# Own bank for turned rows, a bias moved to VectorE, an earlier second routing and earlier keys in the first expert layer

## The reference, cut to what matters

```python
xf = layernorm(x).reshape(-1, 128)                       # 4096 tokens
scores = sigmoid(xf @ Wg.T + bg + bias)                  # 8 experts
top_scores, top_idx = top_k(scores, 2)
h  = gelu(einsum('td,ehd->teh', xf, W1) + b1)            # hidden 512
eo = einsum('teh,edh->ted', h, W2) + b2
shared = gelu(xf @ Ws1.T + bs1) @ Ws2.T + bs2            # every token
x = x + shared + (eo weighted by the two scores)
...
kh = (ctx_1024 @ Wk + bk)                                # next layer's keys, 1601 rows a batch
```

## Time and profile before

| | us |
|---|---|
| median of 3 runs | 1750.25 (1744.02 to 1752.11) |
| the profiled execution, its own time | 1747.45 |
| its span | 1745.6 |
| layer B's front and shared expert | about 150 to 249 |
| the 46 units | about 249 to 490 |
| mean granted TensorE clock | 0.963 of full |

### The profile page before, as it was taken

The page is one execution under the profiler, slowest core; times in us unless marked ns, Lnnn a source line. Parts: engine busy times, 40 slices in busy tenths (PEclk is TensorE's granted clock), DMA queues, the critical chain, the costliest instruction groups (busy, mean ns, idle before and its releaser), DMA issues.

```text
span 1745.6 us, 44990 instructions
## 1 busy us (share of the span) xinstructions
PE 1508.3 (86%) x18392; PEld 923.6 (53%) x18392; DVE 1098.5 (63%) x2790; ACT 1255.9 (72%) x1537; POOL 353.3 (20%) x280
## 2 busy tenths in 40 slices
PE   3537987787789999999999999999988999999996
PEld 2436876676654545555454555445444555545553
DVE  6987245655554565667656465755578777778763
ACT  0453233443379999999999999999985677677664
POOL 7451754011050020201102020000001111221121
PEclk9767999998999999999999999999999999999998
DMA  8402112152233344434423343343200000000000
GB/s 306 149 1 68 52 55 65 49 127 58 56 86 74 72 105 92 93 84 91 95 65 80 91 105 90 74 90 68 83 4 1 7 1 7 7 7 7 7 1 13
DMA packets 71950, 112.75 MB, mean 65 GB/s; under 512 B 14656, under 2 KB 56896, under 8 KB 71360
## 3 DMA queue, kind: packets, MB, share of 16 engines
q1 hardware_dynamic: 65600, 95.09, 22.2%
q0 software_dynamic: 6144, 14.76, 2.7%
HBM read 41.36 MB, written 18.35 MB: 34 GB/s over the span
## 4 chain that ended last, share of the span: by engine, by line
PE 40%; ACT 23%; issue 14%; DVE 11%; POOL 1%; DVEq 1%; ACTq 0%; POOLq 0%
ACT C_probs L2195 20%; PE C_ps_s L1406 7%; PE C_ps_s L1415 7%; PE C_ps_s L858 6%; DVE C_den_t L2367 3%; PE C_ps_o L2090 3%; PE C_ps_o L1431 2%; PE C_ps_s L824 2%; PE C_ps_p L1396 2%; PE C_ps_s L2075 2%; ACT B_hidden L927 2%; PE C_ps_s L845 2%; POOL C_o_t L2240 1%; PE C_ps_s L813 1%; PE C_ps_p L2032 1%
## 5 line engine op out<-in xcount | busy, mean ns | idle before, releaser
L2195 ACT ACTIVATE C_probs<-C_ps_s 128x1024 f32<-128x1024 f32 x832 | 772.2, 1065 | 28.8 <-PE C_ps_s L2075 25.8
L2090 PE MATMUL C_ps_o<-C_probs,C_values 128*16 128x256 f32 x6656 | 440.0, 382 | 7.5 <-DVE C_o_t L2363 6.9
L1494 ACT ACTIVATE D_hidden<-C_ps_s,D_b_up 128x1024 f32<-128x1024 f32 x256 | 275.4, 1114 | 135.6 <-PE C_ps_s L1406 135.4
L2075 PE MATMUL C_ps_s<-C_queries,C_keys 32*128 32x256 f32 x3328 | 211.4, 328 | 26.8 <-ACT C_probs L2195 25.6
L2090 PEld LDWEIGHTS C_ps_o<-C_probs,C_values 128*16 128x16 f32 x6656 | 154.5, 95 | 145.8 <-ACT C_probs L2195 9.9
L2075 PEld LDWEIGHTS C_ps_s<-C_queries,C_keys 32*128 32x128 f32 x3328 | 126.8, 183 | 155.4 <-ACT C_probs L2195 117.7
L1406 PE MATMUL C_ps_s<-D_up_in,D_w_up_r 128*128 128x512 f32 x512 | 186.5, 446 | 2.0 <-ACT D_hidden L1494 2.0
L2240 POOL TENSOR_TENSOR C_o_t<-C_o_t,C_den_t 128x512 f32<-128x512 f32 x32 | 40.9, 1277 | 696.9 <-DVE C_den_t L2367 696.9
L858 PE MATMUL C_ps_s<-B_w_dn,B_hidden 128*128 128x128 f32 x736 | 100.5, 294 | 55.2 <-DVE B_unit_lo L1079 35.8
L1509 POOL TENSOR_TENSOR D_gated<-D_gated,D_gated 128x1024 f32<-128x1024 f32 x32 | 76.3, 2383 | 323.5 <-DVE D_gated L1634 323.5
L1415 PE MATMUL C_ps_s<-D_hidden,D_w_down 128*32 128x512 f32 x1024 | 137.7, 610 | 0.8 <-ACT D_hidden L1494 0.8
(11 more groups left out here) (309 smaller groups left out, 2302.2 us busy)
## 6 DMA issues: line engine op xcount, KB each, us to landing
C_keys<-C_k_hi SPq DMA_DIRECT2D x128, 200.1 KB, 4.1
C_ctx_t<-ctx_t_dram SPq DMA_DIRECT2D x16, 800.5 KB, 4.4
C_keys<-C_k_lo SPq DMA_DIRECT2D x64, 200.1 KB, 4.1
B_sorted_rows<-B_zeros SPq DMA_DIRECT2D x2, 2944.0 KB, 14.7
B_unit_in<-B_sorted_rows SPq DMA_DIRECT2D x46, 128.0 KB, 2.4
B_result_rows<-B_unit_out SPq DMA_DIRECT2D x46, 128.0 KB, 1.8
C_queries<-C_q_hi SPq DMA_DIRECT2D x128, 32.0 KB, 1.9
B_w_up<-L_ffn_w_up_dram SPq DMA_DIRECT2D x1, 2304.0 KB
```

The lines of the kernel that those rows point to most:

```text
L1494: nc.scalar.activation(hidden[:, u % RING, :, :], ps_u[u % 2][:], ACT.Gelu, bias=b_up[:, u % PAIRS:u % PAIRS + 1]).then_inc(s_hid, 1)
L2075: m = T.matmul(ps_s[bank(k, 2 * step + j // 2)][:, j % 2, i, :], keys[rows, parity, g, kt * P:(kt + 1) * P], queries[rows, parity, g, :], ...
L2090: m = T.matmul(ps_o[32 * j:32 * j + 2 * DK, g % 2, :], values[:, parity, kt, g * HG + j, :], probs[:, slot(parity, 2 * step + j // 2), j % ...
L2195: nc.scalar.activation(probs[:, slot(parity, n)], ps_s[bank(k, n)][:], ACT.Exp, scale=SCORE_SCALE1).then_inc(s_exp, 1)
```

## The change

Four things. (1) Turned rows of a unit go to the routing bank `ps_g`, and `turn_unit(v)` waits until VectorE has read unit v-1's; `down(v)` loses its wait on `s_us`, and its result moves to the free half of the bank. (2) `down_shared` loses the bias product; `add_shared` adds the bias on VectorE before it waits for the result. (3) Turned blocks 1 and 2 go to the two halves of `ps_s[2]`, `xt` has four places instead of two, the turns of blocks 4 to 7 come one block earlier, and so do their scores, ahead of `up_shared`; the second half's `choose` and `assign` come earlier on VectorE, and its `ranks` ahead of block 7's `up_shared`. `xt` and `unit_in` now share memory, so the first load of a unit waits for the last split and scores. (4) The key jobs move: 0 and 1 behind `down_shared(5)` and `(6)`, 2, 3 and 4 ahead of the units, 5 and 6 in units 2 and 3.

```diff
-    xt = over["keys1"]("xt", [P, 2, BT, P])
+    xt = [over[place](f"xt{i}", [P, BT, P]) for i, place in enumerate(("keys1", "keys1", "queries", "queries"))]
...
-    ps_t = ps_p[:].rearrange("p (i t) -> p i t", i=BT)
+    ps_t = [bank.rearrange("p (i t) -> p i t", i=BT) for bank in (
+        ps_p[:], *(ps_s[2][:, i].rearrange("p b q -> p (b q)") for i in range(2)))]
...
+            if v == 0:
+                sp.wait_ge(s_logit, BLOCKS)
+                sp.wait_ge(s_parts, BLOCKS)
...
             for i in range(BT):
                 for c in range(CH):
-                    T.matmul(ps_e[k % 2][:, i, :], hidden_s[:, (k + 1) % 2, c, i * P:(i + 1) * P],
-                             w_down[:, SHARED, c, :], start=(c == 0), stop=False)
-                m = T.matmul(ps_e[k % 2][:, i, :], ones[0:1, :], b_down[0:1, SHARED, :], start=False, stop=True)
+                    m = T.matmul(ps_e[k % 2][:, i, :], hidden_s[:, (k + 1) % 2, c, i * P:(i + 1) * P],
+                                 w_down[:, SHARED, c, :], start=(c == 0), stop=(c == CH - 1))
...
         def turn_unit(v):
             pe.wait_ge(s_in[v % 4], 16 * (v // 4 + 1))
-            if v < 2:
-                pe.wait_ge(s_x2, BLOCKS - 1 + v)
-            wait(pe, s_y, v - 3)
+            if v == 0:
+                pe.wait_ge(s_slots, PARTS0)
+            wait(pe, s_us, v)
             for i in range(2):
-                tr = T.transpose(ps_s[2][:, v % 2, 0, i * P:(i + 1) * P], unit_in[:, v % 4, i, :], ident[:])
+                tr = T.transpose(ps_g[:, i * P:(i + 1) * P], unit_in[:, v % 4, i, :], ident[:])
...
             wait(pe, s_y, v - 1)
-            if v + 2 < NV:
-                pe.wait_ge(s_us, v + 3)
+            if v < 2:
+                pe.wait_ge(s_x2, BLOCKS - 1 + v)
...
-        turn_block(0)
-        for k in range(1, BLOCKS // 2):
+        for k in range(3):
             turn_block(k)
-            logits(k - 1)
-        logits(BLOCKS // 2 - 1)
+        logits(0)
+        turn_block(3)
+        for k in range(1, 4):
+            logits(k)
         pe.wait_ge(s_const, CONSTS)
         for k in range(BLOCKS):
+            if 2 <= k < 6:
+                logits(k + 2)
+            if k == 7:
+                ranks(1)
             up_shared(k)
-            if k in (1, 7):
-                ranks(k // 7)
-            if k in (3, 4, 5):
-                logits(k + 1)
-            if k in (2, 3, 4, 5):
-                turn_block(k + 2)
+            if k == 1:
+                ranks(0)
+            if 1 <= k < 5:
+                turn_block(k + 3)
             if k > 0:
                 down_shared(k - 1)
-            if k == 5:
-                logits(7)
-
+            if k >= 6:
+                beside(k - BLOCKS)
+        down_shared(BLOCKS - 1)
+        beside(0)
         turn_unit(0)
+        beside(1)
...
         def add_shared(k):
+            to = x_sb[:, k * BT:(k + 1) * BT, :]
+            chain.mark(V.tensor_tensor(to, to, b_down[:, SHARED:SHARED + 1, :].to_broadcast([P, BT, D]), ALU.add))
             dve.wait_ge(s_down, k + 1)
-            to = x_sb[:, k * BT:(k + 1) * BT, :]
+            chain.settle()
             V.tensor_tensor(to, to, ps_e[k % 2][:], ALU.add).then_inc(s_x2, 1)
...
+        scores(1)
         add_shared(4)
-        scores(1)
         choose(1)
         add_shared(5)
+        beside(-2)
         assign(1)
         tabulate(1)
         add_shared(6)
+        beside(-1)
+        add_shared(7)
+        beside(0)
         prepare(0)
-        add_shared(7)
+        beside(1)
...
-        FIRST_AT = {**{8 + i: i for i in range(len(KEY_AT))}, 31: 7, 32: 8, 33: 9, 34: 10, 35: BEFORE_SCORES}
+        FIRST_AT = {-2: (0,), -1: (1,), 0: (2, 3), 1: (4,), 2: (5,), 3: (6,), 31: (7,), 32: (8,), 33: (9,), 34: (10,),
+                    35: (BEFORE_SCORES,)}
```

More of the change, by code:

```diff
@@ L628 @@
     s_tables: object
+    s_xt: object
     s_ys: list
@@ L728, in expert_layer, with turned_in @@
     CONSTS = 16 * 5
+    def turned_in(k):
+        return ps_t[k if k < 3 else 0]
     def gelus_to(v):
@@ L891, in on_tensor @@
             up(v)
-            down(v - 1)
-            beside(v)
+            if v > 0:
+                down(v - 1)
+                if v > 1:
+                    beside(v)
         return lambda: down(NV - 1)
@@ L934, in on_scalar @@
             gelus_shared(k)
-            if 2 <= k < 6:
-                turned(k + 2)
-            if k == 6:
+            if 1 <= k < 5:
+                turned(k + 3)
+            if k == 5:
                 sigmoid(1)
```

80 lines of the change are left out of this document (39 added, 41 removed).

## The result

The changed kernel takes 1676.45 us, the median of 4 runs (1675.32 to 1680.26), against 1750.63 us for the kernel before beside it: a ratio of 0.9593, 95% interval 0.9564 to 0.9622. On a second chip it took 1676.86 us (5 runs) against 1754.55: 0.956, 0.9544 to 0.9576. The forecast was 1683, the range 1668 to 1704.

What follows compares the result with a forecast made beforehand. It took VectorE's round trip to bound the units and TensorE the shared expert. Units -48.9, bias -18.8, front -0.7, start +2.2 gave -66.2 us from 1747.45: 1681.3 profiled, forecast 1683, range 1668 to 1704.

Steps and rivals of the forecast that it cites:

- The unit loop: Plain units: without the wait in `down`, TensorE bounds them; 4.37 to 3.48 us each, 25 us over 28 units.
- SyncE's queue: Units 18 to 21, which place keys: late row loads keep them near 4.3 us, 3.2 us lost.
- GpSimd's fill: In the units: the fill of the keys still holds one VectorE instruction; gain 1.4 us.
- Long units: Seven intervals with other VectorE work: 1.4 us gained each, 9.8 together, plus 4 from clock in four of them.
- The keys: Key jobs moved out of units 8 to 14, two returning in units 2 and 3: net gain 11.9 us.
- The shared bias: `down_shared` without bias products: 2.35 us gained in each of 8 blocks, 18.8 us; VectorE's additions hidden.
- the low end of 13.1: Bias in `down_shared`: only 0.41 us saved for each tile, 1.64 for each block, 13.1 us.
- The rival that the pair is cheap: Bias pair in `down_shared` costs no more than another pair of passes: 7.0 us gained, 1695 us; chance 0.03.
- Order and start: Ahead of the units: +2.2 us besides the bias, from `down_shared(4)` to `down(0)`; 0.7 us saved in the front.
- A unit partly bound elsewhere: Units: VectorE's spare time used up or rows late, so 3.9 us a unit, 1701 us; 1692 to 1712, chance 0.18.
- a wait that only moves: Units: `turn_unit` waits as long for `s_us` as `down` did, loop stays 4.37 us; 1728 us, chance 0.03.
- a series of transpose and split: Units: with one bank, turns and splits run in series, 5.9 us a unit; 1794 us, chance 0.01.

Runs made afterwards that it cites:

- wait_back: The changed kernel with `down(v)` waiting again for VectorE's reads of unit v+2's turned rows, the separate bank kept: 1723.77 us.
- bank_only: The kernel before with only the turned rows in routing's bank, results in the third score bank, and the waits that go with this: 1699.62 us.
- keys_again: The changed kernel with the seven key jobs back in units 8 to 14, run a second time: 1672.25 us beside 1676.86 on one chip.
- bias_ident: The changed kernel with the shared bias on TensorE as products of the 128-row identity, no bias addition on VectorE: 1681.09 us.
- bias_back: The changed kernel with the shared bias again as four one-row products in each `down_shared`, no bias addition on VectorE: 1693.52 us.
- fill_spread: The changed kernel with GpSimd's fill cut into eight pieces between token tiles of the second scatter: 1673.66 us.

## Why the prediction was right, step by step

The forecast came out 6.5 us too high; the sign, the size and the main mechanism held, and one term, the keys, was wrong. The trace gives 4.2 of the 6.5 to the units (53.1 measured, 48.9 forecast). By its own sum the forecast would have been 1681.3 + 2.8 = 1684 and not 1683. By its steps:

*The unit loop.* The mechanism stands: one loop through VectorE, cut by the wait (wait_back, bank_only). The plain unit was put at 3.48 us and is 3.41; the 0.21 for the transposes is 0.14 (288.36 to 288.50). The prediction took it as the difference between a down that had waited and one that had not, and the first is itself slower: 1.86 us to the next work with the wait (wait_back, 288.25 to 290.11) and 1.78 without (286.58 to 288.36). Over 28 plain units that is 2 us.

*The whole of the units*, forecast -48.9, measured -53.1 in the profiled execution. SyncE's queue was put at 3.2 us lost, measured 3.2. GpSimd's fill was to give 1.4; its unit went from 11.02 to 6.28 us, of which the unit behind it, at low clock, takes 1.5 back, so it gave some 3. That is luck: the fill had been running for 1.6 us when VectorE came to the copy that it holds, and TensorE waits 2.5 us there, not 5.7 as in the earlier trace rows. In the second execution the copy is held for 5.34 us, the two units take 7.07 and 6.19, and the gain is 1.2. Long units gained 17.0 against 13.8 forecast with their clock. But in this execution the low clock moved into the unit behind (unit 31 takes 5.21, unit 40 5.33), which the prediction had as plain. Together the eleven intervals gained 16.8 where 9.8 + 4 + 4 x 0.89 = 17.4 was expected. Right in sum, by two errors that cancel, and so by luck.

What the prediction gave to the wait alone, 25 + 6.2 + 9.8 + 4 + 1.4 - 3.2 = 43.2, was too little: bank_only has 51.8 in its 44 units.

*The keys.* This is the step whose name was wrong. Its 11.9 us is the whole gain of units 8 to 14 less the return of two jobs. 7 x 0.89 = 6.2 of it came from the wait, and so would have come without any move; it was even more (bank_only has the key units at 4.14 instead of 5.37, and the last at 6.46 instead of 9.10: 10.0 in all at full clock). What was left for the move, 5.7, is what 4.2 us of added work at the start had to be set against, a net gain of 1.5. The 4.2 was about right (4.3); the 5.7 should have been 3.65, five jobs at 0.73, and the chip shows a net loss of 4.6 (keys_again). The cause is in the prediction's own words: it says that TensorE's own products are on the path instead, and then books the job as saved in the units and cheap ahead of them. With TensorE the bound on both sides, a job moved from one to the other saves nothing, and ahead of the units VectorE's round trips come on top (waits of 1.8 and 0.6 us in the stretch from 205.2 to 237.4, where the granted clock is 0.89).

*The shared bias.* -18.8 was right (2.32 measured for a block, eight blocks, 17.8 at result 0), the low end of 13.1 was not needed. Its reason, a price for each change of kind, is now shown, with one thing put right: not any change of the stationary operand has it (bias_ident), only a change of the row count. The rival that the pair is cheap was rightly held to be improbable; it would be true of a pair of 128 rows.

*Order and start.* From the end of `down_shared(4)` to the end of `down(0)` 38.3 - 7.1 + 2.2 = 33.4 us was forecast, 32.2 measured (205.2 to 237.36), with the low clock still in it. The 0.7 us in the front did not come: `up_shared(0)` starts 0.85 earlier, at 161.13, but at low clock, and routing's ranks stand where they did, 169.44 against 169.49.

*The rivals.* A unit partly bound elsewhere (3.9), a wait that only moves and a series of transpose and split are all refuted by 34.53 busy us of 34.60.

What is left open is the routing in blocks 1 to 5 and the order at the units' start, which were not run by themselves. By medians, 51 us by the bank alone and 17 for the bias make 68, and with the keys at a loss of 4.6 some 11 to 14 of the 74 to 78 us are left for them, give or take the few us between chips. Two kernels that ran on one chip differ in just this part and the keys: bias_back is bank_only with them. It is 6.1 us faster by the medians, so some 11 without the keys' loss, but the executions overlap (1690.81 to 1700.02 against 1696.77 to 1707.19). At result 0 it is 2.1 us ahead (255.47 against 257.59), which with the keys' 3.5 makes some 6. The other 5.0 lie in the units (175.71 against 180.69 us), where both have the same loop and differ by where the low clock and the late rows fall. So about 6 us is what the traces support. bank_only shows a wait of 2.7 us for VectorE's split ahead of its first unit that the changed kernel does not have in that form; that is a hint, not a proof.

## What to carry to other kernels

When a wait is taken off a loop that several stages share, book the gain of every iteration to the wait first, and only what is left to the other parts; otherwise a part that loses, like the early keys here, looks as if it paid. Work moved within a stretch that the same engine bounds saves nothing, while work of another engine should be cut into pieces no longer than that engine's idle time in one iteration. On TensorE, a lone product with fewer rows among full ones is worth replacing by one with all rows if no other engine can take it.

## What the runs showed of the hardware

A product of 1 or of 64 rows (two passes here) among products of 128 costs 0.39 us more than one of 128 rows, 0.2 at each change, and the loss shows as a late weight load (0.31 us behind the last one, not 0.11). I had expected the price to belong to any product with another stationary operand.

GpSimd's fill of 5.45 us holds a copy of VectorE within SBUF from the moment the copy is asked for to the end of the fill (4.15 for 0.43 us). It does not hold everything: the result of a unit, which VectorE takes from PSUM, needs its usual 0.42 us at 263.87, while the fill runs. In the kernel before, shows an instruction that reads PSUM as held, but a copy within SBUF stood ahead of it, and the two records end together (timeline of VectorE, kernel before):

```profile
278.27 5.49 DVE L1074 COPY B_b_unit<-B_b_up 128x4 f32 x1
```

The Trainium skill ("SBUF — State Buffer", section on the two separate sides) calls the port pair that both share an exclusive lock, held for a whole instruction; the trace agrees for the copy. fill_spread shows that with eight fills of 0.78 us the units from 5 to 8 take 3.42 to 3.80.

TensorE's granted clock was lower behind some of the gaps, and where the low stretch lies decides whether it costs anything. Table by stretch of the changed kernel, columns as in the earlier trace rows: unit 7 with the fill, unit 8 behind it, unit 30 with its statistics, unit 31 behind it.

```profile
263.87:270.15 6.28, 3.77 (x31) 3.49 (x30) 5.91 (x7) 2.78 (x6) 4.62 (x1) 0.94 0.16 42
270.15:275.02 4.87, 4.87 (x33) 4.72 (x32) 2.17 (x8) 1.68 (x4) 0.00 (x0) 0.73 0.21 57
351.78:358.16 6.38, 4.22 (x32) 3.67 (x32) 5.65 (x28) 2.19 (x5) 4.86 (x6) 1.00 0.34 95
358.16:363.37 5.21, 5.07 (x33) 4.88 (x36) 2.51 (x9) 1.70 (x5) 1.17 (x2) 0.68 0.28 79
```

The units behind run at 0.73 and 0.68 (a mix of the levels 1.2 and 2.4 GHz), busy throughout, and take 1.5 us more. In the other profiled execution of the same kernel the low stretch lies in the long unit itself:

```profile
352.00:358.00 6.00, 4.99 (x28) 4.81 (x29) 5.33 (x26) 1.68 (x4) 4.48 (x6) 0.72 0.31 87
358.50:362.00 3.50, 2.75 (x23) 2.43 (x22) 3.43 (x11) 1.77 (x5) 1.98 (x3) 1.00 0.37 94
```

There unit 30 takes 6.38 us all the same, since VectorE bounds it, and unit 31 takes 3.77: the low clock cost next to nothing, 0.36 us at most. Such differences of 1.5 us a place are part of what the executions of one kernel differ by.
